# Flamingo two-layer kernel: first loads in pieces, six K/V units ahead of the tokens, blocks split sooner

## What is computed

```python
x = x + tanh(g_xattn[0]) * L0_xattn(layernorm(x), ids, ctx, ctx, ctx)   # gated unit whose expert (weights: one batch of ctx) is picked by token id
x = x + tanh(g_ffn[0])   * L0_ffn(layernorm(x), w_gate, w_up, w_down)   # ternary weights, 8-bit tokens, Hadamard transform
x = x + tanh(g_xattn[1]) * L1_xattn(layernorm(x), ctx, Wq, Wk, Wv, Wo)  # 16 heads of 128, keys and values from ctx
x = x + tanh(g_ffn[1])   * L1_ffn(layernorm(x), ...)                    # 32 routed experts, 8 per token, and a shared one

# the part of layer 1 on which the change works: keys and values need only ctx and the weights
k = (ctx @ Wk).reshape(b, skv, 16, 128)
v = (ctx @ Wv).reshape(b, skv, 16, 128)

# the 8-bit tokens of L0_ffn
scale = 128 / clip(max(abs(x), axis=-1), 1e-5)
xq = clip(round(x * scale), -128, 127) / scale
```

## Time and profile before

| | |
|---|---|
| time, median of 3 runs | 571.99 us (571.52 to 573.06) |
| profiled execution | 570.56 us, span 568.8 us |
| PE busy | 536.6 us (94%) |
| DVE, ACT, POOL busy | 387.8, 351.6, 319.4 us |
| chain that ended last | PE 71%, DVE 9%, POOL 7%, ACT 5%, DMA 4%, issue 3% |
| PE clock | full but for slices in which it had been idle |

### The profile page before, as it was taken

One profiled execution on the slowest core, in us unless ns is written; L12 is line 12 of the kernel. 1 busy time (PEld: TensorE's weight loads), 2 busy tenths in 40 slices (PEclk: granted clock), 3 DMA queues, 4 the chain that ended last, 5 costly groups with the idle time before them and its releaser, 6 DMA issues.

```text
span 568.8 us, 9603 instructions
## 1 busy us (share of the span) xinstructions
PE 536.6 (94%) x3232; PEld 462.1 (81%) x3232; DVE 387.8 (68%) x818; ACT 351.6 (62%) x723; POOL 319.4 (56%) x318
## 2 busy tenths in 40 slices
PE   3999998998999999999999999999999899879997
PEld 3777766776878988999999999999898788668886
DVE  4867987589956576556555576656665867857882
ACT  3651144566478687666666655756766666677882
POOL 3579037899448797655553424335687445852320
PEclk9999998999999999999999999999999999989999
DMA  8901135610047767578795768534454645355651
GB/s 280 356 20 53 42 109 170 201 39 1 20 171 224 236 189 219 170 256 256 231 302 185 250 201 238 181 124 148 139 188 151 206 162 177 97 142 169 222 176 39
DMA packets 66672, 95.78 MB, mean 168 GB/s; under 512 B 6336, under 2 KB 38848, under 8 KB 66624
## 3 DMA queue, kind: packets, MB, share of 16 engines
q1 hardware_dynamic: 66624, 95.17, 52.8%
HBM read 67.23 MB, written 27.92 MB: 167 GB/s over the span
## 4 chain that ended last, share of the span: by engine, by line
PE 71%; DVE 9%; POOL 7%; ACT 5%; DMA 4%; issue 3%; SPq 1%; DVEq 0%; POOLq 0%; ACTq 0%
PE ps L1535 20%; PE ps L1536 19%; PE ps L1537 19%; PE ps L1640 4%; PE ps L1745 2%; PE ps L1729 2%; DMA k_hl<-k_scratch 2%; DMA xr<-in_x 1%; PE ps L1752 1%; ACT q2T L910 1%; DMA cw_row<-cw_scratch 1%; PE ps L1758 1%; POOL kv_w_lo L573 1%; ACT kv_w_hi L815 1%; POOL s_lo L655 1%
## 5 line engine op out<-in xcount | busy, mean ns | idle before, releaser
L650 POOL TENSOR_TENSOR probs<-probs,rsum 128x512 f32<-128x512 f32 x64 | 66.4, 1042 | 59.6 <-DVE rsum L1241 59.6
L1236 DVE TENSOR_REDUCE nmax<-ps 128x2 f32<-128x512 f32 x64 | 44.1, 689 | 35.0 <-PE ps L1537 34.6
L1034 ACT ACTIVATE e_hi<-e_r 128x512 fp32r<-128x512 f32 x64 | 40.3, 630 | 32.6 <-DVE e_r L1461 31.8
L948 ACT ACTIVATE probs<-ps,nmax 128x256 f32<-128x256 f32 x128 | 59.8, 481 | 1.0 <-DVE nmax L1236 0.8
L573 POOL TENSOR_TENSOR kv_w_lo<-blk_raw,kv_w_hi 128x1024 fp32r<-128x1024 f32 x16 | 38.9, 2432 | 38.3 <-ACT kv_w_hi L815 38.3
L1461 DVE SCALAR_TENSOR_TENSOR e_r<-ps,cw_row 128x512 f32<-128x512 f32 x64 | 43.6, 686 | 17.0 <-PE ps L1537 16.0
L1227 DVE TENSOR_TENSOR pT_lo<-ps,pT_hi 128x512 fp32r<-128x512 f32 x64 | 43.8, 686 | 11.6 <-ACT pT_hi L954 10.9
L1232 DVE TENSOR_TENSOR oT_lo<-ps,oT_hi 128x512 fp32r<-128x512 f32 x32 | 22.1, 692 | 40.2 <-ACT oT_hi L958 40.2
L769 POOL TENSOR_TENSOR e_lo<-e_sq,e_hi 128x512 fp32r<-128x512 f32 x19 | 24.5, 1291 | 43.8 <-ACT e_sq L1040 41.4
L954 ACT ACTIVATE pT_hi<-ps 128x512 fp32r<-128x512 f32 x64 | 38.3, 600 | 16.5 <-PE ps L1640 16.3
L958 ACT ACTIVATE oT_hi<-ps 128x512 fp32r<-128x512 f32 x32 | 19.1, 597 | 40.9 <-PE ps L1537 40.9
(11 more groups left out here) (292 smaller groups left out, 1868.6 us busy)
## 6 DMA issues: line engine op xcount, KB each, us to landing
cw_row<-cw_scratch SPq DMA_DIRECT2D x64, 256.0 KB, 3.5
v_hl<-v_scratch SPq DMA_DIRECT2D x24, 512.0 KB, 3.5
blk_raw<-in_w_blocks SPq DMA_DIRECT2D x23, 512.0 KB, 4.5
k_scratch<-kv_out SPq DMA_DIRECT2D x32, 256.0 KB, 2.9
v_scratch<-kv_out SPq DMA_DIRECT2D x32, 256.0 KB, 3.2
k_hl<-k_scratch SPq DMA_DIRECT2D x14, 512.0 KB, 3.6
v_scratch<-kv_hi SPq DMA_DIRECT2D x24, 256.0 KB, 2.5
blk_raw<-in_w_tail SPq DMA_DIRECT2D x10, 512.0 KB, 4.8
```

Source lines behind the costliest of these rows:

```text
L650: nc.gpsimd.tensor_tensor(probs[:, b, :, :], probs[:, b, :, :], rsum[:, b, :].unsqueeze(2).to_broadcast([P, 2, S]), ALU.mult).then_inc(pro ...
L948: last = nc.scalar.activation(probs[:, b, t, :], ps[:, S_BANK[b], t * S:(t + 1) * S], ACT.Exp, bias=nmax[:, b, t:t + 1], accum_out=esum[:, ...
L1034: nc.scalar.activation(e_hi[i % 4][:, :], e_r[i % 2][:, :], ACT.Square).then_inc(e_hi_done, 1)
L1236: V.tensor_reduce(nmax[:, b, :], ps[:, S_BANK[b], :].rearrange("p (t k) -> p t k", t=2), AX.X, ALU.max, negate=True).then_inc(max_done, 1)
```

## The change

- SP loads block 0's first quarter (keys of head 0), then the two context chunks of half 0 singly, then the other three quarters, then x and the rest as before. ACT copies these pieces one by one. DVE makes the low part of each context chunk of half 0, POOL now that of half 1 (`ctx_late_done`), ahead of the masks.
- The first eight units (`first_keys`) order their matmuls high x high, low x high, high x low, with a wait for each piece.
- s0 has six units instead of three, f1 one instead of two. `FRONT_UNITS` becomes 28; every later slot holds later units, and m19 and e19 are empty. In ACT's list the copies of units 0 to 5 stand together, with the high parts of context half 1 between the second and the third.
- ACT makes block 1 ahead of the first Silu, block 2 where block 1 was, block 3 where block 2 was, block 4 in step 1 as before, none in step 0. POOL makes block 1 ahead of the ternary weights and no longer waits for `scales_ready` ahead of block 2.
- DVE adds tile 0's experts between the product that gives z of half 1 and its low part.
- `quantise` folds two small operations and, for half 1, uses a scalar_tensor_tensor with a broadcast constant.
- Q0's transposes take the bank first whose unit was copied first, with a wait for each.

```diff
-        FILLS = {"s0": 3, "s1": 1, "a11": 1, "y2": 1, "y6": 4, "u0": 2, "g1": 1, "u1": 3, "f0": 3, "g2": 1, "f1": 2, "d4": 0, "d5": 1, "c6": 1, "d6": 2}
+        FILLS = {"s0": 6, "s1": 1, "a11": 1, "y2": 1, "y6": 4, "u0": 2, "g1": 1, "u1": 3, "f0": 3, "g2": 1, "f1": 1, "d4": 0, "d5": 1, "c6": 1, "d6": 2}
...
-            load_context(0)
-            load_block(0)
+            sp.dma_start(blk_raw[0][:, 0:D], w_blocks[0, 0, :, 0:D]).then_inc(ld_keys[0], 16)
+            for c in range(DC):
+                sp.dma_start(cT_raw[:, c, 0:GT], ctx_t[c * P:(c + 1) * P, 0:GT]).then_inc(ld_ctx[c], 16)
+            sp.dma_start(blk_raw[0][:, D:4 * D], w_blocks[0, 0, :, D:4 * D]).then_inc(ld_keys[1], 16)
             sp.dma_start(xr[:, 0:GN, :], x[0:GT, :].rearrange("(n p) d -> p n d", p=P)).then_inc(ld_x[0], 16)
             sp.dma_start(eye[:, :], ident_in).then_inc(ld_const, 16)
-            load_context(1)
+            sp.dma_start(cT_raw[:, :, GT:T], ctx_t[:, GT:T].rearrange("(c p) n -> p c n", p=P)).then_inc(ld_ctx[2], 16)
...
+            for c in range(DC):
+                pool.wait_ge(ctx_hi_done, DC + c + 1)
+                nc.gpsimd.tensor_tensor(cT_lo[:, c, GT:T], cT_raw[:, c, GT:T], cT_hi[:, c, GT:T].bitcast(F32), ALU.subtract)\
+                    .then_inc(ctx_late_done, 1)
             pool.wait_ge(ld_ids, 32)
...
+            block_low(1)
             for i in range(3):
-                if i == 2:
-                    block_low(1)
                 pool.wait_ge(wscale_done, 1)
...
-            pool.wait_ge(scales_ready, 1)
             block_low(2)
             block_low(3)
...
+            def take_unit(k):
+
+                act.wait_ge(kv_filled, k + 1)
+                if k >= 4:
+                    act.wait_ge(kv_stored[k % 4], 16 * stores_into(k % 4, k - 1))
...
-            take("s0")
...
+            act.wait_ge(ld_keys[1], 16)
+            nc.scalar.activation(kv_w_hi[0][:, D:4 * D], blk_raw[0][:, D:4 * D], ACT.Copy).then_inc(first_keys_hi_done, 1)
+            for k in FILL_AT["s0"]:
+                if k == 2:
+                    act.wait_ge(ld_ctx[2], 16)
+                    for c in range(DC):
+                        context_high(c, 1)
+                take_unit(k)
             for c, (filled, done) in enumerate(((first_T_filled, first_hi_done), (hT_filled, hT_hi_done))):
...
+            block_high(1)
             for g in range(NG):
                 if g:
                     first_expert(g)
                     take("a11")
-                    block_high(1)
+                    block_high(2)
...
-            block_high(2)
+            block_high(3)
...
-                if i < 2:
-                    block_high(3 + i)
+                if i == 1:
+                    block_high(4)
...
                 V.tensor_tensor(a_sel[:, g, :, :], a_sel[:, g, :, :], a_silu[:, :, :], ALU.mult).then_inc(z_ready, 1)
+                if g:
+                    add_experts([0])
                 dve.wait_ge(z_hi_done, g + 1)
...
-            for n in range(GN):
-                add_experts([n], n - 1 if n else None)
+            for n in range(1, GN):
+                add_experts([n], n - 1)
...
+            def first_keys(k, n, g):
...
+                pe.wait_ge(first_keys_hi_done, 1 if n == 0 else 2)
+                for c in range(DC):
+                    pe.wait_ge(ctx_hi_done, g * DC + c + 1)
+                    mm(ps[:, fill_bank(k), :], kv_w_hi[0][:, at[c]], cT_hi[:, c, tokens], start=(c == 0), stop=False)
...
-                        elif b == 4:
-                            pe.wait_ge(kv_taken, FILL_AT["y6"][-1] + 1)
...
-                    for c in range(DC):
+                    chunks = range(DC) if n else [fill_bank(k) - b for k in FILL_AT["y6"][-2:]]
+                    for c in chunks:
+                        if n == 0:
+                            pe.wait_ge(kv_taken, FILL_AT["y6"][-2:][chunks.index(c)] + 1)
```

## The result

The changed kernel takes 582.73 us (median of 6 runs, 579.41 to 586.07) against 572.52 (6 runs, 568.64 to 574.49): a ratio of 1.0189, 95% interval 1.0159 to 1.0219. Forecast were 581.9 and slower; the store wait in the opening and the wait in m0 are both there, at nearly the size forecast. Parts 2 and 3 did not come as reasoned, and what the sum of the parts had too much was made up by a slow stretch of the clock that no part had.

What follows compares the result with a forecast made beforehand. PE was taken as the bound, busy 94% of the span and 99.79 of 100 us in attention. Terms 11.6 - 0.2 - 0.4 - 2.0 - 0.6 + 4.3 - 2.8 = +9.9 on 571.99 gave 581.9 us, range 576.5 to 586.

Steps and rivals of the forecast that it cites:

- Parts 2 and 3: Expert stage: earlier block 1 delays e = 2 of half 1, +0.8; tile 0 added ahead of z_lo saves 1.0 us.
- Part 1: Opening: with six early fill units, the fifth copy waits for store 0 to land, delaying e = 0: +11.6 us.
- Parts 4 to 6: Q0's reordered transposes -0.4; F0's shorter idle and full clock, less a block 4 wait, -2.0; f1 with one unit -0.6.
- part 5: F0: chain and POOL earlier, idle 2.12 to 1.2 us, no slow clock, less a wait for block 4: -2.0 (rounded).
- Part 7: m0: its unit waits for block 8's split, +2.65, then runs at half clock, +1.6: +4.3 us.
- Part 8: Attention: two units fewer (m19, e19) where PE is the bound: -2.8 us.
- (a): Opening: no wait for the stores, 570.5 us, or 566.2 if m0's block is ready too; chance 7%.
- (b): Opening: a store lands 2.0 us after its issue, at 20.4 instead of 25.3: 577.0 us; chance 4%.
- (c): m0 costs nothing because block 8 is split in time: 577.6 us; chance 9%.
- (d): Clock also falls at the idles of 1.2 us (F0) and 1.5 us (before Q1): 585.1 us; chance 10%.

Runs made afterwards that it cites:

- e19: Not a run: a slot for a fill unit in attention, left empty by the change; no time of its own.
- e1_free: Changed kernel with ACT's copies of the fifth, sixth and seventh fill units put into idle memory instead of kv_out: 571.21 us, 0.9979 of the kernel before.
- e5_early_stores: Changed kernel with SP issuing the stores of units 0 and 1 ahead of its load of block 1, unit 2's right behind it: 578.14 us (one run).
- e4_old_fills: Changed kernel with the old unit counts (s0 3, f1 2) and blocks 2 and 3 back in their old places on ACT: 575.39 us, ratio 1.0067.
- e9_block1_alone: Kernel before with one edit, ACT making block 1's high part ahead of the first Silu: 572.51 us (one run).
- e7_ctx_dve: e4_old_fills with the low part of context half 1 made by DVE behind its hT_lo, not by POOL: 572.43 us, ratio 0.9997.
- e6_act_queue: Changed kernel with ACT, not SP, issuing the stores of units 0, 1 and 2 right behind each copy: 572.36 us, ratio 1.0008.

## Why the prediction was right, and where it wasn't

**Part 1** (+11.6) held: forecast landing 25.3, e = 0 at 28.75, measured 28.94; e1_free shows the cause. Its assumption on the queue (a store waits for SP's earlier bytes) is shown by e5_early_stores. Wrong in it, without effect: six units end at 17.1, not at 15.3 (the half clock lasts until 12, each pair 1.05 us), and DVE's `h` ends at 16.8, not at 14.9, since POOL's new subtractions hold it. I costed moving that low part from DVE to POOL at nothing, unsaid. Hidden behind the six units, which hold PE until 17.1, and behind the store wait, this step cost nothing here; in e4_old_fills it is what made the kernel slow.

**Parts 2 and 3** (+0.8 and -1.0) were both wrong on their own. The delay of 0.8 us doesn't come, as e9_block1_alone shows: I kept DVE's product at its length of 2.10 us, but that length came of a meeting with POOL, and later it takes 1.23. The gain of 1.0 us is real, and has two sufficient causes, of which I named one. Measured from e = 0 to tile 3: -1.2 us, where I had nothing (-0.2 for the two parts, +0.2 for the tail of the slow clock).

**Parts 4 to 6**: Q0's wait went from 0.69 to 0.25 us. F0's idle is 1.48 us, not 1.2, and the clock stays full behind it, as it does behind 1.42 us before Q1; in e4_old_fills and e7_ctx_dve, with block 3 at its old place, F0 waited 2.3 us and the clock fell. In f0 PE waited 0.38 us for block 4, where I had 0.7. From tile 3 to Q1 the change gained 2.7 us; forecast were 3.0 (the terms of part 5 add up to -1.9, not to the -2.0 written). The shorter `quantise` and the order of Q0 were not tried alone.

**Part 7** (+4.3) held: 4.2 us in the profiled execution, 2.4 for the wait (forecast 2.65), 1.5 for the clock (1.6) and 0.3 before attention. That the clock falls was a chance, though, and I took it for certain: it did in three executions of five with this wait. Where it doesn't, the part is 2.7 us.

**Part 8** (-2.8) held: from 222 to 411 us 190.38 us before, and 187.63 after where both had full clock: -2.75. Ahead of that, from the first transposes of probabilities to 222, there is a gain that no part had: 50.88 us before and 50.23 after. All other kernels, with and without the wait in m0, have 50.2 to 50.5, but for e9_block1_alone, which is as before (50.83); which edit brings it stays open.

**The sum** of 9.9 against 10.04 in the profiled execution is better than its terms: 1.4 us of cost too many up to attention's end were made up by a slow stretch near 480 (1.3) that no step had, and 0.2 behind it. So the closeness of the total is luck in part. The medians are 10.2 us apart.

**Rivals.** (a) and (b) are out: the store landed at 25.6, 6.7 us after its issue at 18.84. (c) is out, the block was late. (d) is out: no fall behind any idle of 1.2 to 1.5 us. The range held the median with 3 us to spare, but the kernel's single runs reach its end (586.07): it had no room for slow stretches without idle, of which each costs 1.3 to 1.7 us.

## What to carry to other kernels

An edit that fills an engine sooner must be followed to the buffers that its output needs: four `kv_out` were enough for three early units, and the fifth waited for the queue's whole backlog. Three copies into idle memory gave the lost 10 us back. Durations taken from a profile for an engine that shares memory with another hold only for that phase: check what the other engine does at the new time. Moving block 8 sooner took a wait of 2.4 us away and cost 0.7 in this way. And when a wait is removed, ask which second edit would have removed it too, before adding both gains.

## What the hardware showed that I hadn't expected

- The granted clock fell to 0.50 for 3 to 4 us with PE busy throughout, between 372 and 390 us in eight of the thirteen profiled executions of this study and between 466 and 484 in eight. Behind the idle of 2.35 us (before 503.04 in the earlier trace rows) it fell in ten of thirteen, behind the 2.46 us of m0 in three of five. Each stretch costs 1.3 to 1.7 us: 189.2 against 187.6 us between the same two points near 222 and 411, 31.2 against 29.8 between those near 459 and 490. The times of e6_act_queue lie mostly in steps, 569 us at a mean clock of 0.997, 572 at 0.991, 574 at 0.988, which fits two and three such stretches more. What sets them off stays open.
- A 256 KB store took 2.0 us alone, 6.4 beside a loaded queue from a queue of its own, and 11.4 behind the same loads in their queue.
